# A selective scan on one core: the sum that ends Softplus and the product dt*u on another engine

## What is computed

```python
xp = x @ W_xproj
dt, Bm, Cm = jnp.split(xp, [DT_RANK, DT_RANK + D_STATE], axis=-1)
dt = jax.nn.softplus(dt @ W_dt + b_dt)
A = -jnp.exp(A_log)
def step(h, inp):                       # over the 64 positions of a window
    dt_t, B_t, C_t, u_t = inp
    dA = jnp.exp(dt_t[:, :, None] * A)
    dBu = (dt_t * u_t)[:, :, None] * B_t[:, None, :]
    h = dA * h + dBu
    y = jnp.einsum('bdn,bn->bd', h, C_t)
    return (h, y)
```

## Time and profile before

| | |
|---|---|
| median of 3 runs | 9865.25 us (9864.34 to 9874.51) |
| the profiled execution | 9872.89 us |
| its span | 9871.1 us |
| instructions | 90850 |
| PE, PEld, DVE, ACT, POOL busy | 62%, 27%, 80%, 40%, 57% |
| HBM traffic | 119 GB/s over the span |

### The profile page before, as it was taken

How to read it: one execution, slowest core, us unless ns; L and a number is a source line. 1 busy time by engine, 2 the same in 40 slices (tenths; PEclk the granted TensorE clock), 3 DMA queues, 4 the chain that set the end, 5 groups by cost and what they waited for, 6 DMA issues and landing times. The chain is left out here.

```text
span 9871.1 us, 90850 instructions
## 1 busy us (share of the span) xinstructions
PE 6166.5 (62%) x28498; PEld 2618.1 (27%) x28498; DVE 7851.4 (80%) x6692; ACT 3981.3 (40%) x4196; POOL 5614.4 (57%) x2056
## 2 busy tenths in 40 slices
PE   6888888888854455555555555555555555555544
PEld 3444444444421111111111111111111111111133
DVE  3555555555559999999999999999999999999933
ACT  1222222222235555455555554555555544555400
POOL 0000000000038888888888888888888888888800
PEclk8888888888877777667676776776776777776766
DMA  0000000000024544454455444544554445444454
GB/s 19 20 18 18 20 20 20 18 18 20 20 83 165 174 165 162 162 176 161 162 170 175 161 162 164 174 161 162 171 174 162 160 156 175 168 162 168 146 148 135
DMA packets 493850, 1202.07 MB, mean 122 GB/s; under 512 B 166357, under 2 KB 168569, under 8 KB 493561
## 3 DMA queue, kind: packets, MB, share of 16 engines
q1 hardware_dynamic: 493305, 1201.13, 36.5%
q0 software_dynamic: 512, 0.53, 0.0%
HBM read 943.42 MB, written 231.21 MB: 119 GB/s over the span
## 5 line engine op out<-in xcount | busy, mean ns | idle before, releaser
L926 POOL TENSOR_TENSOR b_h<-b_h,b_ct 128x896 f32<-128x896 f32 x1792 | 4948.2, 2782 | 905.6 <-DVE b_h L1082 876.6
L1082 DVE TENSOR_TENSOR_SCAN b_h<-b_a,b_h 128x896 f32<-128x896 f32 x1792 | 3600.6, 2009 | 0.0
L1011 ACT ACTIVATE b_a<-b_dts,decay 128x882 f32<-128x882 f32 x1792 | 1781.1, 998 | 2878.0 <-DVE b_h L1082 2792.3
L1076 DVE TENSOR_TENSOR b_h<-b_dus,b_bt 128x896 f32<-128x896 f32 x1792 | 2405.3, 1342 | 218.0 <-DMA b_dus<-d_dtu 216.3
L1197 PE MATMUL b_y<-b_h,fold 128*32 128x512 f32 (+1 forms) x7168 | 1191.1, 804 | 1165.3 <-POOL b_h L926 1165.3
L931 POOL MEMSET b_seq<- 128x938 f32 x2 | 1.7, 880 | 2762.0 <-POOLq L761 2762.0
L469 DVE TENSOR_TENSOR a_xg<-a_xn,a_pb 128x784 f32<-128x784 f32 x512 | 495.9, 969 | 628.3 <-PE a_pb L583 628.3
L1166 PE MATMUL b_w<-b_seq,w_conv 128*128 128x384 f32 (+1 forms) x896 | 516.0, 733 | 660.0 <-DMA b_seq<-b_seq 658.9
L592 PE MATMUL a_pa<-a_xg,w_exp 128*128 128x512 f32 (+1 forms) x2048 | 927.4, 581 | 0.0
L1197 PEld LDWEIGHTS b_y<-b_h,fold 128*32 128x32 f32 x7168 | 241.4, 143 | 1989.2 <-POOL b_h L926 1436.0
L1158 PE MATMUL b_w<-b_u,w_dt_full 128*128 128x512 f32 x448 | 365.0, 968 | 530.1 <-ACT b_u L948 529.1
(11 more groups left out here) (204 smaller groups left out, 8075.8 us busy)
## 6 DMA issues: line engine op xcount, KB each, us to landing
b_bt<-d_rows SPq DMA_DIRECT2D x448, 448.0 KB, 4.3
b_ct<-d_rows SPq DMA_DIRECT2D x448, 448.0 KB, 3.7
b_dts<-d_dt SPq DMA_DIRECT2D x448, 448.0 KB, 6.0
b_dus<-d_dtu SPq DMA_DIRECT2D x448, 448.0 KB, 7.1
d_dt<-b_dt SPq DMA_DIRECT2D x112, 448.0 KB, 2.5
d_dtu<-b_soft SPq DMA_DIRECT2D x112, 448.0 KB, 2.5
b_seq<-b_seq SPq DMA_DIRECT2D x112, 234.0 KB, 7.5
a_x<-in_x SPq DMA_DIRECT2D x64, 392.0 KB, 3.2
```

The costliest lines, as they stand in the source:

```text
L926: nc.gpsimd.tensor_tensor(hh[t][:], hh[t][:], ct[t // 4 % 2][:], ALU.mult).then_inc(hc_done, 1)
L1011: a(steps(aa[t % 2]), steps(dts[t % 4]), ACT.Exp, scale=decay[:, t % 4, t // 4:t // 4 + 1]).then_inc(a_done, 1)
L1076: v.tensor_tensor(hh[t][:], dus[t % 4][:], bt[t // 4 % 2][:], ALU.mult).then_inc(b_done, 1)
L1082: v.tensor_tensor_scan(hh[t][:], aa[t % 2][:, 0:TB], hh[t][:], 0.0, ALU.mult, ALU.add).then_inc(h_done, 1)
```

## The change

GpSimd's `products` is dropped, and its two operations go to VectorE as `softplus_sum` and `dt_input`, with the same operands, shapes and semaphores. The sum stands after input product t=7 and scan t=6, the product after input product t=8 and scan t=7, in each of the 111 units that prepare a next one. In the prologue both stand behind the first sequences. The waits of SyncE and ScalarE on `dt_ready`, `dtu_ready` and `l_ready` are as they were.

```diff
@@ -911,25 +911,15 @@
 
                     @block.gpsimd
                     def _(pool):
-                        def products(j, o):
-
-                            pool.wait_ge(l_ready, o)
-                            nc.gpsimd.tensor_tensor(dtb[:], dtb[:], soft[:], ALU.add).then_inc(dt_ready, 1)
-                            pool.wait_ge(dt_ready, o)
-                            nc.gpsimd.tensor_tensor(soft[:], dtb[:], u[j][:], ALU.mult).then_inc(dtu_ready, 1)
-
                         def unit(i, it, kind):
                             for t in range(UNIT):
                                 if t % 4 == 0:
                                     pool.wait_ge(ct_in[t // 4 % 2], it * 64 + (32 * i + 16 * (t // 8)))
                                 pool.wait_ge(h_done, tile_no(i, t, it))
                                 nc.gpsimd.tensor_tensor(hh[t][:], hh[t][:], ct[t // 4 % 2][:], ALU.mult).then_inc(hc_done, 1)
-                                if t == 5 and not (kind == LAST and i == 1):
-                                    products(1 - i, unit_no(i, it) + 1)
 
                         for i in range(2):
                             nc.gpsimd.memset(seq[i][:], 0.0).then_inc(pads_zero, 1)
-                        products(0, 2)
                         unit(0, 1, FIRST)
                         unit(1, 1, FIRST)
                         with pool.Fori(2, N) as it:
@@ -1103,6 +1093,14 @@
                             dve.wait_ge(gate_ready, o)
                             v.tensor_tensor(yz[j][:], yy[:, 0:TB], gate[j][:], ALU.mult).then_inc(yz_ready, 1)
 
+                        def softplus_sum(o):
+                            dve.wait_ge(l_ready, o)
+                            v.tensor_tensor(dtb[:], dtb[:], soft[:], ALU.add).then_inc(dt_ready, 1)
+
+                        def dt_input(j, o):
+                            dve.wait_ge(dt_ready, o)
+                            v.tensor_tensor(soft[:], dtb[:], u[j][:], ALU.mult).then_inc(dtu_ready, 1)
+
                         def residual(c, q):
                             dve.wait_ge(made, c + 2)
                             dve.wait_ge(x3_stored, 16 * q)
@@ -1121,6 +1119,11 @@
                                     scan((t - 1) % UNIT, tile_no(i, t, it) - 1)
                                 if t == 4 and not (kind == FIRST and i == 0):
                                     gated(1 - i, row_no(i, 0, it) - 1, unit_no(i, it) - 1)
+                                if not (kind == LAST and i == 1):
+                                    if t == 7:
+                                        softplus_sum(unit_no(i, it) + 1)
+                                    if t == 8:
+                                        dt_input(1 - i, unit_no(i, it) + 1)
                                 if i == 0 and kind != LAST:
                                     if t == 11:
                                         norm(spot(0, "xc", it, kind), it + 1)
@@ -1136,6 +1139,8 @@
                         dve.wait_ge(pads_zero, 2)
                         norm(START.index("xc"), 1)
                         sequences(None, 1)
+                        softplus_sum(2)
+                        dt_input(0, 2)
                         unit(0, 1, FIRST)
                         unit(1, 1, FIRST)
                         with dve.Fori(2, N) as it:
```

## The result

The changed kernel takes 10408 us (median of 4 runs, 10401.69 to 10419.49) against 9866.47 before: a ratio of 1.0549, 95% interval 1.053 to 1.0567. The forecast was 10406, its range 10300 to 10530. The profiled execution has a span of 10406.2 us, 535.1 more than before.

A forecast was written before the change was run, and what follows sets the result against it. VectorE, busy 96% of the second phase, was taken as the bound. 641.6 - 98.5 - 2.1 = +541.0 us on the median 9865.25 gave 10406 us (+5.5%), range 10300 to 10530.

The forecast's parts named there:

- The bound: Second phase: VectorE, busy 6236 of 6510 us (96%), sets its length; GpSimd is not the late engine.
- Part 1: Two VectorE insertions per unit, each 0.98 us itself plus GpSimd's exclusive 1.91 us turn: 222 x 2.89 = 641.6 us.
- Part 2: Input product behind the sequences, first unit of each pair: GpSimd, relieved, is up to date; 1.79 us less, 55 times, 98.5 us.
- the two extra turns: GpSimd operations let in ahead of input products t=8 and t=9, 1.91 us each, helping GpSimd catch up before the sequences.
- The gate: Gated product L1104: less GpSimd arrears may spare 0.2 us every second unit, 11 us, costed at nothing.
- Part 3: Waits and queues: logarithm wait has 8 us slack, SyncE delays nothing behind it, load wait stays near 181 us; cost nothing.
- Part 4: Prologue: two GpSimd operations of 2.08 us become about 1.06 us each on VectorE, -2.1 us.
- Rival A: New operations bring no GpSimd turn, so an insertion costs 0.98 us: +117, 9982 us; chance 8%.
- rival B: Long input products come from GpSimd's lag and vanish with two operations less per unit: -388, 9477 us; chance 4%.
- rival C: GpSimd is still one operation behind at the sequences, so nothing is gained there: +639.5, 10505 us; chance 10%.
- rival D: The added operations fit into VectorE's existing waits, so nothing measurable changes; chance 1%.

The follow-up runs named there:

- e_adjacent: Changed kernel with the dt*u product directly behind the sum, both after scan t=6: 10194.86 us, ratio 1.0329.
- e_sum_only: Changed kernel with only the sum on VectorE, the product staying on GpSimd behind hc t=6: 10087.64 us, ratio 1.0219.
- e_psum: Changed kernel with sum and product reading ScalarE's decay tile in PSUM in place of dt: 10227.2 us, ratio 1.037.
- e_no_hc: Changed kernel with GpSimd's product with C done on 8 of 896 columns only: 9550.09 us, ratio 0.9676.
- e_drop: Kernel before, with GpSimd's sum and product on 8 of 896 columns and nothing added to VectorE: 9812.06 us, ratio 0.9943.
- e_add_tiles: Changed kernel plus a full-size spare sum and product on GpSimd in the old place, each reading two different tiles: 10399.49 us, ratio 1.0525.
- e_add: Changed kernel plus a full-size spare sum and product on GpSimd in the old place, each reading one tile twice: 10539.57 us, ratio 1.0675.

## Why the prediction was right

- *The bound.* VectorE sets the phase: it kept 9 tenths throughout, and the phase grew by what was added to its queue, though GpSimd had 710 us less to do.
- *Part 1, 222 x 2.89 = 641.6.* Measured: 639 us over all 222 insertions, 2.88 each; scan to scan is 5.80 us with one and 2.92 without. The number, the place and the condition were each tested alone (e_adjacent, e_sum_only, e_psum, e_no_hc), and came out within some 15 us of what was expected.
- *Part 2, -98.5.* It is there, with 96.8 us: the input product behind the sequences has a mean of 1.09 us in the changed kernel, and in e_drop it has 1.09 too. But the prediction gave it to the removal "and the two extra turns"; e_add_tiles shows that the extra turns alone do it, and e_drop that the removal alone does it too. Either was enough.
- *The gate, costed at nothing with 11 us in the range.* Its wait is 20 us less, and from scan to scan its place in the first unit of a pair is 12.5 us less in all, so the 11 belonged into the sum. This is most of why the phase grew by 526 us and not by 543.
- *Part 3.* No wait for the logarithm within the loop, the load wait at 179 us, SyncE's queue within 0.1 us of the working.
- *Part 4, -2.1.* From the sum's start to the first scan it was 17.8 us and is 15.7.
- Rival A fell with the input products at t=8 and 9 of the changed kernel, rival B with the time and with e_drop, rival C with the short input product behind the sequences, rival D with the time.

That the total came within 2 us of the forecast is in part luck. The sum is 17 us too high for the stretch of the scans. Outside of it the profiled executions differ by +9 us, where -2 was forecast, which makes up 11; and the profiled execution before was 6 us slower than the median (9872.89 against 9866.47), which makes up the rest.

The page "SBUF — State Buffer" of the Trainium skill (who interferes with whom) sets two SBUF inputs as the condition for a VectorE instruction; e_psum agrees: behind an operation with one input in PSUM the input product takes 2.20 us in place of 2.96. It speaks of the whole instruction as the loser's wait; at 2.96 us less 1.06 that is 1.90, nearer to the 1.91 taken than to 2.08.

## What to carry to other kernels

Before moving an elementwise operation between VectorE and GpSimd, look at what stands next to it: an operation of two SBUF inputs on VectorE cost 0.98 us here where it stood alone between two scans, and 2.88 where it stood ahead of another of its kind, with a GpSimd operation in between. Put such operations in one pile, not one per step; here that, together with the loads it released earlier, was worth 2.4%. A pile costs more turns when GpSimd enters it behind. An engine with idle time in the totals can still be late at one point of an in-order queue, so read who waits for that instruction, and what is queued behind the one who waits.

## What the runs showed that I had not expected

- GpSimd's sum and product of 128 x 896 fp32 took 2.56 and 2.41 us where both inputs were the same tile, 2.95 and 2.80 with two tiles, in the same place. Why was not tried.
- Shorter GpSimd operations made VectorE slower in two places. They shift GpSimd's step against VectorE's, and a VectorE operation that used to find it done finds it running: 44 us in e_drop, 134 in e_add. The even rhythm of 2.92 us seems to rest on GpSimd's turn (about 1.9) fitting almost exactly under the scan (1.93 from its start to the next product); no run varied the length of either to show it.
